# Turning the activated x tiles by DMA: 16-bit halves split on GpSimd, stored, and read back transposed

## The chip, the core and the metric

The kernel runs on one core of one Trainium2 chip. The metric is the device time in microseconds (us) of one execution. The kernel before takes 1605.04 us (median of 3 runs, 1604.93 to 1605.71).

## The reference, cut to what matters

The program is one layer: a layer norm, a state space mixer with a residual, a second layer norm, and a dense product with low-rank experts and a residual. Tokens: 2 batches of 512. The mixer has 128 heads of 64 features in 8 groups, and works in 4 chunks of 128 tokens.

```
proj = einsum('bsd,ed->bse', x, in_proj_w)          # gate | x, B, C | dt
hBC  = silu(causal depthwise conv with 4 taps(x, B, C))
xch  = hs * dt                                      # chunked, hs is the x part of hBC
Y_diag = einsum('bzlhn,bzshn,bhzls,bzshp->bzlhp', Cc, Bc, L, xch)
states = einsum('bzlhn,bhzl,bzlhp->bzhpn', Bc, decay_states, xch)
Y_off  = ...the states carried from chunk to chunk...
y = Y_diag + Y_off + hs * D ;  g = y * silu(gate) ; rms norm per group ; out projection
```

`proj` comes out with features on partitions and tokens along the row, since the convolution runs over tokens. `xch` is contracted over tokens, so `hs` has to be turned (tokens on partitions) before both `Y_diag` and `states`.

## The kernel before, in words

After a prologue of some 67 us the mixer runs 64 units, `k = 8 g + j`: group `g` of 8, unit `j` of 8, each unit 128 features (two heads) for both batches `b`. Every engine has its own instruction list, written out in order; semaphores join them. Each unit works one step ahead: while unit `k` is finished, the convolution of unit `k + 1` is made.

TensorE, in the order of its list for unit `k` (`body`, lines 878 to 955): the out products of banks 2 and 3 of unit `k - 1` (`later_outs`), the x projection of unit `k + 1` (`project` into `x_bank`), the chunk states of unit `k` (`states`, which wait for `xdecay`), the diagonal products (`diagonal`, which wait for `scores` and `xdt`), the gate projection of `k + 1`, the carried part (`carry`, which waits for `state`), the out products of banks 0 and 1 (which wait for `conv_ready` of unit `k + 1`), in units 4 and 5 of a group a projection of the next group's B or C, and then `turn_hs`: four 128 x 128 transposes for each batch, of `hs` of unit `k + 1`, into `head_bank`. The projections use products of a high and a low part, three for one.

VectorE, in the order of its list (`body`, lines 1357 to 1412): `to_heads` for both batches (line 1278: `xdt` is the turned `hs` times dt; it waits for `turned` and stands first in the unit), `add_outs` and the two `score` products, `y_low_part`, in units 1 to 3 `normed_out` (8 of them in a group), `tap(1)`, `carried_state` for both batches, `tap(2)` and `tap(3)` (which give `conv_ready` for unit `k + 1`), then `skip`, `carry_part`, `add_carry` (which give `y_sum`), and `add_outs`. In units 5 and 6 the taps of the next group's B and C (`bc_tap`) stand behind the first `add_outs`, and the scores of these units are made at the end of the unit before.

ScalarE: `tap0`, the high parts of the weights (`high_part`), the decays of the scores, `silu_hs` (line 1045: `hs_ready` for unit `k + 1`), the two gate activations, `finish`. In units 4 and 5 there is a third weight tile, whose high part stands behind the gate activations.

GpSimd: `decayed` for both batches (line 1469: `xdecay` from `xdt`), the low parts of the weights (line 1448), `add_squares`, the low part of the out weights, further low parts, and last `gated` for both batches, which waits for `y_sum`.

The SP queue issues every DMA, in the order of its list (`body`, lines 713 to 753): a weight tile, the out weights of unit `k + 1`, tables and columns in some units, weight tiles, `load_sums` for both batches, weight tiles, and `load_grown` (four DMAs, which wait for `y_sum` of unit `k`).

## Time and profile before

| what | value |
|---|---|
| median of the runs | 1605.04 us |
| span of the profiled execution | 1605.0 us |
| TensorE busy | 1583.5 us, 99% |
| VectorE busy | 1264.2 us, 79% |
| ScalarE busy | 1163.1 us, 72% |
| GpSimd busy | 700.7 us, 44% |
| DMA: mean busy share of 16 engines by the SP queue | 30.8% |

The profile is one execution. "Busy" is the time in which an engine has at least one instruction under way. The chain that ended last is followed back from the last instruction; its shares say which engine set the time. A timeline row gives the start in us from the span's start, the time from there to the end of the merged instructions, the engine, the line and operation, and in brackets how long the engine sat idle before it and who released it.

### The profile page before, as it was taken

The page shows a single profiled execution, that of the slowest core. Times are in us where ns is not written, and L with a number is a line of the kernel's source. Part 1 is how long each engine was busy: PE and PEld are TensorE (multiplying, and loading weights), DVE is VectorE, ACT ScalarE, POOL GpSimd, SP SyncE. Part 2 cuts the span into 40 slices and gives each one's busy share as a digit, 9 for nine tenths or more (in the row PEclk, how much of TensorE's full clock was granted, in tenths as well). Part 3 has the DMA queues.
Part 4 walks back from the last instruction along what each step waited for, and adds up shares of the span by engine and source line. Part 5 has one row for each costly group of instructions (what it writes and reads, how often), then busy time and mean ns, then how long its engine had stood idle before and what let it go on. Part 6 is the DMA issues. An engine that isn't in the chain of part 4 may idle for free.

```text
span 1605.0 us, 26714 instructions
## 1 busy us (share of the span) xinstructions
PE 1583.5 (99%) x9576; PEld 1346.1 (84%) x9576; DVE 1264.2 (79%) x1984; ACT 1163.1 (72%) x2027; POOL 700.7 (44%) x535
## 2 busy tenths in 40 slices
PE   7899999999999999999999999999999999999998
PEld 5688888888888888888888888888888888888887
DVE  6687777877778777887778877787877878788787
ACT  5887667776777677777687766777677767777753
POOL 2155444453444454354453544445344445435550
PEclk9999999999999999999999999999999999999999
DMA  4542322332323233332232232233232323223211
GB/s 151 192 145 86 122 89 83 112 112 73 112 97 114 73 109 95 98 106 92 99 108 97 86 122 89 83 112 112 73 112 99 113 73 109 99 92 112 93 44 53
DMA packets 86916, 162.37 MB, mean 101 GB/s; under 512 B 23040, under 2 KB 39424, under 8 KB 86528
## 3 DMA queue, kind: packets, MB, share of 16 engines
q1 hardware_dynamic: 86784, 160.66, 30.8%
q8 instruction: 77, 1.26, 0.3%
q14 instruction: 55, 0.45, 0.1%
HBM read 154.84 MB, written 5.77 MB: 100 GB/s over the span
## 4 chain that ended last, share of the span: by engine, by line
PE 97%; DVE 1%; ACT 1%; issue 0%; DMA 0%; SPq 0%; DVEq 0%; ACTq 0%
PE g_bank L778 10%; PE g_bank L780 9%; PE g_bank L779 9%; PE d_bank L797 7%; PE x_bank L778 7%; PE x_bank L780 7%; PE x_bank L779 7%; PE head_bank L786 5%; PE head_bank L804 5%; PE x_bank L836 4%; PE x_bank L837 4%; PE x_bank L835 4%; PE d_bank L837 4%; PE d_bank L835 4%; PE d_bank L836 4%; PE head_bank L812 3%
## 5 line engine op out<-in xcount | busy, mean ns | idle before, releaser
L1448 POOL TENSOR_TENSOR w_low<-raw,w_high 128x512 fp32r<-128x512 f32 x139 | 179.8, 1294 | 553.5 <-ACT w_high L1011 553.5
L1199 DVE SCALAR_TENSOR_TENSOR hs<-x_bank,cols,hs 128x1022 f32<-128x1022 f32 x189 | 241.6, 1278 | 129.7 <-ACT hs L1033 127.5
L1021 ACT ACTIVATE scores<-scores,tables 128x128 f32<-128x128 f32 x1024 | 312.4, 391 | 0.0
L1462 POOL TENSOR_TENSOR y<-y,gate 128x512 f32<-128x512 f32 x128 | 185.4, 1467 | 198.8 <-DVE y L1268 198.8
L1033 ACT ACTIVATE hs<-x_bank,cols 128x1024 f32<-128x1024 f32 x63 | 75.9, 1204 | 269.9 <-PE x_bank L780 269.9
L778 PE MATMUL g_bank<-x_high,w_high 128*128 128x512 f32 x624 | 250.8, 402 | 0.0
L779 PE MATMUL g_bank<-x_low,w_high 128*128 128x512 f32 x624 | 243.2, 390 | 0.0
L780 PE MATMUL g_bank<-x_high,w_low 128*128 128x512 f32 x624 | 243.1, 390 | 0.0
L778 PE MATMUL x_bank<-x_high,w_high 128*128 128x512 f32 x504 | 196.3, 390 | 0.1
L780 PE MATMUL x_bank<-x_high,w_low 128*128 128x512 f32 x504 | 196.1, 389 | 0.0
L779 PE MATMUL x_bank<-x_low,w_high 128*128 128x512 f32 x504 | 196.1, 389 | 0.0
L1231 DVE TENSOR_TENSOR scores<-scores,bc 128x1024 f32<-128x1024 f32 x128 | 169.0, 1327 | 4.3 <-ACT scores L1026 4.3
L778 PEld LDWEIGHTS g_bank<-x_high,w_high 128*128 128x128 f32 x624 | 117.0, 188 | 33.4 <-issue 11.0
L1469 POOL TENSOR_TENSOR xdecay<-xdt,tables 128x384 f32<-128x384 f32 x128 | 109.0, 873 | 78.4 <-DVE xdt L1278 78.4
L780 PEld LDWEIGHTS g_bank<-x_high,w_low 128*128 128x128 f32 x624 | 117.1, 188 | 25.3
L1026 ACT ACTIVATE scores<-scores 128x1024 f32<-128x1024 f32 x128 | 135.8, 1062 | 2.6
L779 PEld LDWEIGHTS g_bank<-x_low,w_high 128*128 128x128 f32 x624 | 117.2, 188 | 22.4 <-issue 0.2
L1456 POOL TENSOR_TENSOR square_sum<-square_sum,gate 128x1024 f32<-128x1024 f32 x55 | 133.0, 2419 | 3.3 <-DVE scores L1231 2.9
L1245 DVE SCALAR_TENSOR_TENSOR state<-state,chunk_tab,head_bank 128x64 f32<-128x64 f32 x512 | 121.0, 278 | 9.1
L797 PE MATMUL d_bank<-scores,xdt 128*64 128x128 f32 x2048 | 126.1, 276 | 0.0
L1256 DVE TENSOR_TENSOR grown_rows<-head_bank,grown_rows 128x384 f32<-128x384 f32 x128 | 71.4, 557 | 64.4 <-PE head_bank L804 57.3
L797 PEld LDWEIGHTS d_bank<-scores,xdt 128*64 128x64 f32 x2048 | 110.5, 137 | 7.9 <-issue 0.2
(211 smaller groups left out, 3433.3 us busy)
## 6 DMA issues: line engine op xcount, KB each, us to landing
scores<-sums_dram SPq DMA_DIRECT2D x128, 512.0 KB, 4.8
raw<-w_in SPq DMA_DIRECT2D x144, 256.0 KB, 2.9
grown_rows<-grown_dram SPq DMA_DIRECT2D x256, 96.0 KB, 2.8
out_raw<-w_out SPq DMA_DIRECT2D x64, 256.0 KB, 3.4
mixed<-x SPq DMA_DIRECT2D x8, 256.0 KB, 5.1
out<-mixed SPq DMA_DIRECT2D x8, 256.0 KB, 2.0
table_dram<-table SPq DMA_DIRECT2D x2, 768.0 KB, 5.3
tables<-table_dram SPq DMA_DIRECT2D x30, 48.0 KB, 2.7
```

What stands on the lines that cost most here:

```text
L778: pe.matmul(to, w_high[:, slot, k], x_high[:, b, k], start=(k == 0), stop=False)
L779: pe.matmul(to, w_high[:, slot, k], x_low[:, b, k], start=False, stop=False)
L780: mm = pe.matmul(to, w_low[:, slot, k], x_high[:, b, k], start=False, stop=(k == KT - 1))
L797: mm = pe.matmul(d_bank[r * HEAD_DIM:(r + 1) * HEAD_DIM, b, c * P:(c + 1) * P], xdt[:, b, c, r], scores[:, s, b, r, c], start=True, stop=True)
L835: pe.matmul(to, y_high[:, q, b, at], out_high[:, q], start=(i == 0), stop=False)
L1021: op = s.activation(at, at, ACT.Relu, bias=col[:, r, c:c + 1], scale=-1.0)
L1026: s.activation(scores[:, q % 2, b], scores[:, q % 2, b], ACT.Exp, scale=-1.0).then_inc(exp_ready, 1)
L1199: v.scalar_tensor_tensor(out=hs[:, q % 2, :, i:], in0=x_bank[:, :, 0:SEQ - i], scalar=cols[:, q, TAPS - 1 - i:TAPS - i], in1=hs[:, q % 2, ...
L1231: v.tensor_tensor(at, at, bc[:, b].rearrange("p c l -> p (c l)").unsqueeze(1) .to_broadcast([P, PAIR, SEQ]), ALU.mult).then_inc(scores_rea ...
L1448: pool.tensor_tensor(w_low[:, slot], raw[:, slot], w_high[:, slot].bitcast(F32), ALU.subtract)\
L1456: pool.tensor_tensor(square_sum[:], square_sum[:], gate[:, q % 2], ALU.add).then_inc(square_added, 1)
L1462: pool.tensor_tensor(y[:, b], y[:, b], gate[:, q % 2, b], ALU.mult).then_inc(y_ready, 1)
```

## The change

The eight TensorE transposes for each unit from unit 1 on are taken out; unit 0 keeps them (`turn_first`). In their place:

- GpSimd copies, behind the low parts of the weights and ahead of `gated`, for each batch the 512 fp32 words of `hs` of unit `k + 1` as two planes of 16-bit halves into `planes` (`planes_of`, 128 x 1024 16-bit elements each).
- SP stores each batch's planes to DRAM (`store_planes`, 256 KB), and after `load_grown` issues for each batch a transposing DMA (`turn_planes`, 256 rows of 512 16-bit elements in, 128 partitions of 4 x 256 out) that writes the turned fp32 words into `xdt`. It waits for the store, for `diag_done` and for `xdecay_ready` of unit `k`.
- VectorE's `to_heads` reads `xdt` and writes it in place; it waits for `xdt_in` and no longer for `turned`.
- `load_out` stands behind the stores and loads the tile for the unit after next.
- The wait for `carry_scaled` moves from `turn_hs` to `states`.
- `bias_high` and `bias_low` lie in space of `x_low` and `x_high` that is free by then; `bias_high` waits for the last projection.

```diff
+            def store_planes(k, b):
+                sp.wait_ge(planes_ready, BATCH * (k - 1) + b + 1)
+                reached(sp, xdt_in[b], 16 * (k - 1))
+                sp.dma_start(planes_dram[b], planes[:, b]).then_inc(planes_stored[b], 16)
+
+            def turn_planes(k, b):
+
+                sp.wait_ge(planes_stored[b], 16 * k)
+                sp.wait_ge(diag_done, BATCH * (k - 1) + b + 1)
+                sp.wait_ge(xdecay_ready, BATCH * (k - 1) + b + 1)
+                sp.dma_start_transpose(xdt[:, b].rearrange("p c r d -> p c (r d)").bitcast(U16),
+                                       planes_dram[b].rearrange("f h t -> (f h) t")).then_inc(xdt_in[b], 16)
...
-                    if ahead:
-                        load_out(ahead[2], (j + 1) % 2)
...
                     if ahead:
                         for b in range(BATCH):
+                            store_planes(ahead[2], b)
+                    if second:
+                        load_out(second[2], j % 2)
+                    if ahead:
+                        for b in range(BATCH):
                             load_grown(ahead[2], b)
+                        for b in range(BATCH):
+                            turn_planes(ahead[2], b)
...
             def states(k, b):
                 pe.wait_ge(xdecay_ready, BATCH * k + b + 1)
+                reached(pe, carry_scaled, BATCH * (k - 1) + b + 1)
...
-                    if ahead:
-                        for b in range(BATCH):
-                            turn_hs(k + 1, (j + 1) % 2, b)
...
             def to_heads(g, q, k, b):
                 if q % HALF == 0:
                     v.wait_ge(tables_in[b][q // HALF], 16 * (g + 1))
-                v.wait_ge(turned, BATCH * k + b + 1)
-                reached(v, diag_done, BATCH * (k - 1) + b + 1)
-                reached(v, xdecay_ready, BATCH * (k - 1) + b + 1)
+                if k == 0:
+                    v.wait_ge(turned, b + 1)
+                    hs_tok = head_bank[b].rearrange("p (c r d) -> p c r d", c=CHUNKS, r=PAIR)
+                else:
+                    v.wait_ge(xdt_in[b], 16 * k)
+                    hs_tok = xdt[:, b]
...
+            def planes_of(k, i, b):
+                pool.wait_ge(hs_ready, k + 1)
+                reached(pool, planes_stored[b], 16 * (k - 1))
+                pool.tensor_copy(planes[:, b], hs[:, i, b].bitcast(U16).rearrange("p (t h) -> p h t", h=HALVES))\
+                    .then_inc(planes_ready, 1)
...
                     for at in splits[1:]:
                         low_part(*at)
+                    if unit(g, last, j + 1):
+                        for b in range(BATCH):
+                            planes_of(k + 1, (j + 1) % 2, b)
                     for b in range(BATCH):
                         gated(j, k, b)
```

## Rows read from the trace of the kernel before

**Rows 1.** The page: busy times; granted TensorE clock, tenths, in 40 slices.
```profile
PE 1583.5 (99%) x9576; PEld 1346.1 (84%) x9576; DVE 1264.2 (79%) x1984; ACT 1163.1 (72%) x2027; POOL 700.7 (44%) x535
PEclk9999999999999999999999999999999999999999
```

**Rows 2.** The page: shares by engine of the chain that ended last.
```profile
PE 97%; DVE 1%; ACT 1%; issue 0%; DMA 0%; SPq 0%; DVEq 0%; ACTq 0%
```

**Rows 3.** Waits of TensorE, longest in total: us, times, longest.
```profile
PE x_bank L273 <- DVE xn L460: 8.6, 3, 5.7
```

**Rows 4.** Timeline of TensorE around the transposes of one unit.
```profile
670.85 1.03 PE L812 MATMUL head_bank<-ident,hs 128*128 128x128 f32 x8
671.64 0.48 PE L835 MATMUL d_bank<-out_high,y_high 128*128 128x512 f32 x1
```

**Rows 5.** Busy time of the engines in one group and in one unit.
```profile
670.85:861.40 190.55, 190.55 (x1168) 162.95 (x1167) 150.88 (x233) 139.99 (x244) 86.16 (x66) 1.00 0.30 99
671.64:693.68 22.04, 22.04 (x139) 18.82 (x138) 18.50 (x31) 16.91 (x31) 10.60 (x9) 1.00 0.30 102
```

**Rows 6.** Timeline of VectorE in that unit, from the end of its first step.
```profile
671.65 1.28 DVE L1278 TENSOR_TENSOR xdt<-head_bank,tables 128x512 f32<-128x512 f32 x2
673.31 0.69 DVE L1300 TENSOR_TENSOR acc<-d_bank,acc 128x512 f32<-128x512 f32 x1 [0.38 <-PE d_bank L837]
...
677.99 2.06 DVE L1304 SCALAR_TENSOR_TENSOR mixed<-acc,g_rstd,mixed 128x512 f32<-128x512 f32 x3
681.35 1.28 DVE L1199 SCALAR_TENSOR_TENSOR hs<-x_bank,cols,hs 128x1022 f32<-128x1022 f32 x1 [1.29 <-ACT hs L1033]
...
684.98 2.59 DVE L1199 SCALAR_TENSOR_TENSOR hs<-x_bank,cols,hs 128x1020 f32<-128x1020 f32 x2
```

**Rows 7.** Timelines of ScalarE and GpSimd in that unit.
```profile
681.22 1.14 ACT L1011 ACTIVATE w_high<-raw 128x512 fp32r<-128x512 f32 x2
...
687.60 1.06 ACT L1045 ACTIVATE hs<-hs 128x1024 f32<-128x1024 f32 x1 [0.52 <-DVE hs L1199]
688.57 1.10 ACT L1053 ACTIVATE gate<-g_bank 128x512 f32<-128x512 f32 x2
...
686.77 1.31 POOL L1448 TENSOR_TENSOR w_low<-raw,w_high 128x512 fp32r<-128x512 f32 x1
```

**Rows 8.** Timeline of the SP queue in that unit: DMA issues.
```profile
683.59 0.91 SPq L682 DMA_DIRECT2D scores<-sums_dram  x2
691.40 2.37 SPq L689 DMA_DIRECT2D grown_rows<-grown_dram  x4
...
694.45 0.43 SPq L678 DMA_DIRECT2D out_raw<-w_out  x1
```

**Rows 9.** DMA issues: count, KB each, median us from issue to landing.
```profile
out<-mixed SPq DMA_DIRECT2D x8, 256.0 KB, 2.0
...
tables<-table_dram SPq DMA_DIRECT2D x30, 48.0 KB, 2.7
```

**Rows 10.** DMA packets in the stretch 759.2 to 760.8 us, nearly all small.
```profile
DMA packets 374, 0.10 MB, mean 64 GB/s; under 512 B 361, under 2 KB 361, under 8 KB 374
...
q1 hardware_dynamic: 374, 0.10, 31.0%
```

**Rows 11.** The page: the SP queue's packets, MB, share of 16 engines.
```profile
q1 hardware_dynamic: 86784, 160.66, 30.8%
```

**Rows 12.** Groups of GpSimd instructions by line: busy us, mean ns.
```profile
L1456 POOL TENSOR_TENSOR square_sum<-square_sum,gate 128x1024 f32<-128x1024 f32 x55 | 133.0, 2419 | 3.3 <-DVE scores L1231 2.9 <-ACT gate L1074 0.4
...
L254 POOL TENSOR_SCALAR_AFFINE_SELECT ident<-ident 128x128 f32<-128x128 f32 x1 | 0.3, 292 | 0.1
...
L250 POOL MEMSET causal<- 128x128 f32 x1 | 0.2, 204 | 0.0
```

**Rows 13.** The engines around TensorE's idle time in the prologue; columns as in rows 5.
```profile
45.00:50.00 5.00, 1.11 (x8) 0.64 (x7) 4.89 (x5) 5.00 (x15) 0.00 (x0) 0.80 0.45 170
50.00:55.00 5.00, 4.81 (x12) 2.98 (x13) 0.52 (x1) 4.54 (x7) 0.00 (x0) 0.51 0.55 154
```

More of the change, by code:

```diff
@@ L9 @@
 F32R = mybir.dt.float32r
+U16 = mybir.dt.uint16
 ALU = mybir.AluOpType
@@ L21 @@
 PAIR = P // HEAD_DIM
+HALVES = 2
 GH = HEADS // GROUPS
@@ L97, in build @@
     dense_dram = scratch("dense_dram", [P, KT * HID])
+    planes_dram = nc.dram_tensor("planes_dram", [BATCH, P, HALVES, SEQ], U16, kind="Internal").ap()
     x_tokens = x.rearrange("b (c p) d -> p (b c) d", p=P)
@@ L134, in build @@
               conv_bc, unit_cols, w_out, bias, dense_dram, sums_dram, grown_dram, table_dram, chunk_dram,
-              out_tokens)
+              planes_dram, out_tokens)
 def prologue(nc, sem, banks, x_high, x_low, mixed, ident, causal, eps_col, buffers, loads, counts, x_tokens, w_dt,
@@ L619, in mixer @@
         chunk_tab = sb("chunk_tab", [P, BATCH, GH, CHUNKS])
+        planes = sb("planes", [P, BATCH, HALVES, SEQ], U16)
         ident_r = sb("ident_r", [P, P], F32R)
-        bias_high, bias_low = sb("bias_high", [P, HID], F32R), sb("bias_low", [P, HID], F32R)
+        bias_high, bias_low = x_low[:, 1, 0], x_high[:, 1, 0]
         g_std, g_rstd, squares = sb("g_std", [P, TB]), sb("g_rstd", [P, TB]), sb("squares", [P, TB])
@@ L626, in mixer @@
         out_raw_in = [sem(f"out_raw_in{i}") for i in range(2)]
+        planes_ready = sem("planes_ready")
+        planes_stored = [sem(f"planes_stored{b}") for b in range(BATCH)]
+        xdt_in = [sem(f"xdt_in{b}") for b in range(BATCH)]
         chunk_in = [[sem(f"chunk_in{b}_{h}") for h in range(2)] for b in range(BATCH)]
@@ L756, in _ @@
             load_out(0, 0)
+            load_out(1, 1)
             for b in range(BATCH):
@@ L806, in carry, with turn_first @@
                 mm.then_inc(carried, 1)
-            def turn_hs(k, s, b):
-                pe.wait_ge(hs_ready, k + 1)
-                reached(pe, carry_scaled, BATCH * (k - 1) + b + 1)
+            def turn_first(b):
+                pe.wait_ge(hs_ready, 1)
                 for c in range(CHUNKS):
-                    mm = pe.transpose(head_bank[b][:, c * P:(c + 1) * P], hs[:, s, b, c * P:(c + 1) * P], ident[:])
+                    mm = pe.transpose(head_bank[b][:, c * P:(c + 1) * P], hs[:, 0, b, c * P:(c + 1) * P], ident[:])
                 mm.then_inc(turned, 1)
@@ L859, in product_of @@
                     pe.wait_ge(bias_low_ready, 1)
-                pe.matmul(to, ident_r[:], bias_high[:], start=True, stop=False)
-                pe.matmul(to, ident_r[:], bias_low[:], start=False, stop=False)
+                pe.matmul(to, ident_r[:], bias_high, start=True, stop=False)
+                pe.matmul(to, ident_r[:], bias_low, start=False, stop=False)
                 pe.wait_ge(xt_ready, tb + 1)
@@ L895, in body @@
                                 pe.wait_ge(bc_ready, 1)
-                                turn_hs(0, 0, 0)
-                                turn_hs(0, 0, 1)
+                                turn_first(0)
+                                turn_first(1)
                     if j == 0:
@@ L1159, in body @@
                         s.wait_ge(bias_in, 16)
-                        s.activation(bias_high[:], bias_row, ACT.Copy).then_inc(bias_high_ready, 1)
+                        s.wait_ge(projected, BATCH * TILES)
+                        s.activation(bias_high, bias_row, ACT.Copy).then_inc(bias_high_ready, 1)
                         s.wait_ge(dense_in, 16)
@@ L1273, in to_heads @@
                     v.wait_ge(tables_in[b][q // HALF], 16 * (g + 1))
-                v.wait_ge(turned, BATCH * k + b + 1)
-                reached(v, diag_done, BATCH * (k - 1) + b + 1)
-                reached(v, xdecay_ready, BATCH * (k - 1) + b + 1)
+                if k == 0:
[4 more added lines that the diff above has]
+                    hs_tok = xdt[:, b]
                 col = table_of(DT, b, q).rearrange("p r c -> p c r")
-                v.tensor_tensor(xdt[:, b], head_bank[b].rearrange("p (c r d) -> p c r d", c=CHUNKS, r=PAIR),
+                v.tensor_tensor(xdt[:, b], hs_tok,
                                 col.unsqueeze(3).to_broadcast([P, CHUNKS, PAIR, HEAD_DIM]), ALU.mult)\
@@ L1498, in _ @@
             pool.wait_ge(bias_high_ready, 1)
-            pool.tensor_tensor(bias_low[:], bias_row, bias_high[:].bitcast(F32), ALU.subtract).then_inc(bias_low_ready, 1)
+            pool.tensor_tensor(bias_low, bias_row, bias_high.bitcast(F32), ALU.subtract).then_inc(bias_low_ready, 1)
             for k in range(KT):
```

2 lines of the change are left out of this document (1 added, 1 removed).

## The prediction, made before the changed kernel ran

> **What bounds the kernel now.** I read the page first, then the chain, then the timelines of one ordinary unit. TensorE is busy for 99% of the span at a granted clock of full speed in every slice [rows 1]; the chain that ended last lies on it for 97% [rows 2], and its longest wait in total, 8.6 us in three times, is for the prologue's norm [rows 3]. So in the 64 units each microsecond taken off TensorE counts, until something else is late. A group of 8 units takes 190.55 us, an ordinary unit 22.04 us, with TensorE busy in all of it and VectorE in 18.50 [rows 5]. The other engines wait for TensorE somewhere in each unit. What the reader should look for is how much room they have: the change sends the step from `hs` to `xdt` on a longer way, and this step closes a loop over GpSimd, SP, the DMA engines and VectorE.
>
> **What is removed.** The eight transposes of a unit start at 670.85 and the next product starts at 671.64 [rows 4]: 0.79 us of TensorE. They go from 63 units: 63 x 0.79 = 50 us. If nothing else were late, a unit would take 22.04 - 0.79 = 21.25 us, and the kernel 1605.0 - 50 = 1555. The profiled span and the median of the runs are the same to 0.1 us, so the sums below stand against both.
>
> **What is added, and where it lies.** In the kernel before, `hs` of unit k + 1 is ready at the end of line 1045 at 688.66 [rows 7], and TensorE turns it only at the end of the unit, some 4 us later; that wait costs nothing. After the change `xdt` of k + 1 is ready only after a chain of work, and `to_heads` stands first in VectorE's list: all that VectorE does for the unit (the scores, then `y_low`, the taps, the states) is queued behind it, GpSimd's `xdecay` waits for it, and TensorE's `states` and `diagonal` for both. The taps give `conv_ready`, without which there is no `hs` for the next unit. So there is a loop, from the end of one unit's `to_heads` to the end of the next one's, and its length is a floor under the unit. Its terms:
>
> (a) VectorE from the end of `to_heads` to the end of `tap(3)`, without its idle time: 673.31 to 677.99 is 4.68, and 681.35 to 687.57 is 6.22 [rows 6]: 10.9 us.
>
> (b) `silu_hs`, 1.06 [rows 7]; 1.1 with its start.
>
> (c) The copies on GpSimd, two, of 1024 elements each. No row has such a copy. From above: the sum of two operands of 1024 elements takes 2.42 us. From below: a memset of 128 elements takes 0.204 and the affine select, which reads one operand, 0.292 [rows 12]; eight times as many elements are at most 8 times that, and without the fixed part seen in the smallest instructions (about 0.1, an estimate) they give 0.95 and 1.65 for 1024. I take 1.4, between these two, since a copy reads one operand and does less than a select: 2.8 us for both. GpSimd is free then: its last low part ends at 688.08 [rows 7], so in an ordinary unit (c) starts at once. `gated`, queued behind it, waits for `y_sum` anyway.
>
> (d) SP's queue from the second store on: its issue 0.45 (half of two at 0.91), the out weights 0.43, then the four issues of `load_grown`, 2.37 [rows 8]: 3.25 us. These are ahead of the first transposing DMA. The second store needs 2.0 us to land (256 KB, `out`) [rows 9] and is hidden behind the 2.8 us that follow its issue. `y_sum`, for which `load_grown` waits, comes some 3.3 us after `tap(3)` by the same unit's order and is no later than the planes.
>
> (e) The two transposing DMAs. A small load (48 KB) lands 2.7 us after its issue [rows 9]. Their data: I assume packets of 256 bytes, a quarter of the 1024-byte rows that are read, since a transposing read has to be cut somewhere; then each DMA has 1024 packets, 64 to an engine. In a stretch with nearly only small packets, 374 took 31.0% of 16 engines in 1.6 us [rows 10]: 0.310 x 16 x 1.6 / 374 = 21 ns each, so 64 x 21 ns = 1.35 us. Over the whole span a packet took 0.308 x 16 x 1605 / 86784 = 91 ns, and a megabyte 49 us of one engine [rows 11]; by bytes 256 KB are 0.8 us, by packets at 91 ns 5.8 us. The two share the 16 engines, so the second lands at about 2.5 + 2 x 1.35 = 5.2 us after the first is issued. I take 1.35, since rows 10 is the nearest in packet size; 0.8 and 5.8 are the ends.
>
> The sum is 10.9 + 1.1 + 2.8 + 3.25 + 5.2 + 0.64 + 0.1 = 24.0 us. That is over 21.25 and over 22.04: TensorE is no longer the bound, and the 0.79 us taken off it are idle time.
>
> To a group this adds what VectorE or GpSimd puts into the loop in single units. `normed_out`: 8 x 0.69 = 5.5 [rows 6]. The reduction of the squares and the keeping of B times C: two operations of 1024 elements, 2.3 (by the 1.22 to 1.28 of VectorE's other operations of this size). In units 5 and 6 three taps of 1.25 come in and two scores of 1.15 go out of the loop: 2 x 1.4 = 2.8. In units 4 and 5 the third weight tile's low part is queued ahead of `planes_of` on GpSimd, and its high part on ScalarE behind the two gate activations: 1.1 + 0.6 + 1.3 = 3.0, and in unit 5 one activation of 1.0 more: 7.0 for both [rows 7]. A group is 8 x 24.0 + 5.5 + 2.3 + 2.8 + 7.0 = 209.6 us against 190.55: 19 more. Eight groups: 152. The first unit and the last have no such step, and the last group no B and C ahead, though its units before were the short ones too: about 5 less. 1605 + 152 - 5 = **1752 us**.
>
> **Edits at nothing.** `load_out` a unit earlier takes its load off nobody's path, since its issue stays in (d). The wait for `carry_scaled` at `states` is met: `carry_part` is over a whole projection earlier. The biases' new place costs at most the wait for the last projection, far ahead of the end product. The DMA engines: the stores by 33 MB and the reads by 33 MB on top of 160.66 [rows 11], 126 x 1.35 and 126 x 0.8 us, 17% of the span beside 30.8%; only collisions at the moment of (e) matter, and `load_grown` and the out weights are under way then, which can add some tenths.
>
> **Rivals.**
>
> 1. *TensorE stays the bound*: faster, 1555. The loop with 64 x 2.75 us less would fit 21.25. It needs both copies and both transposing DMAs in 2.8 + 2.7 - 2.75 = 2.75 us together, that is 0.7 us for a copy and 0.7 for a transposing DMA. The lower ends (0.95 and 0.8) give 3.5, and a group then gains 16 of the 19 us back: 1752 - 64 x 2.0 = 1624, still slower. For it: a copy of 16-bit elements may be quicker than rows of fp32 say; part of a batch's data may land beside the other's fixed time. Against it: every bound of (c) and (e) would have to be off at once. Chance 0.12.
>
> 2. *The transposing DMAs are far slower than plain ones of that packet size*: the upper end of (e), 5.8 us for each, adds 2 x 4.45 to each loop, 64 x 8.9 = 570: 2320 us. It decides from about 2.5 us a transposing DMA, where the total passes 1900. For it: the average packet of this trace costs 91 ns [rows 11], and the issue of such a DMA on SP may itself take longer than 0.45 us. Against it: most of these packets are 2 KB and more, and the small ones took 21 ns [rows 10]. Chance 0.17. The page on the three transpose paths is the one that speaks for it.
>
> 3. *TensorE's clock falls.* In the prologue TensorE was busy for 1.11 of 5 us, and the granted clock went to 0.80 and, in the next 5 us with work to do, to 0.51 [rows 13], about the level of 1.2 GHz. With a loop of 24.0 and 21.25 us of work, TensorE idles for some 3 us a unit, in one or two pieces at `states` and at the out products. If each brings 5 us at half the clock, 2.5 us of work are lost a unit, which the 2.75 us of idle time nearly cover; with the units' extras uncovered up to 64 x 2 = 130 us are added: 1880. Chance 0.07. The Trainium skill, page TensorE: Matmul & The Clock Gate, section Why this matters for your kernels, warns of idle gaps of this order between bursts; in rows 13 the trace agrees with it for a gap of nearly 4 us.
>
> 4. *The change does not do what it says*: the transposing DMA is written out as a copy of single elements, 131072 for a batch. At 21 ns over 16 engines that is 172 us a batch, and the kernel takes over 20 ms. Chance 0.01.
>
> **How the numbers follow.** The loop of 24 us has 0.61, rival 1 0.12, rival 2 0.17, rival 3 0.07, rival 4 0.01, and 0.02 is for a loop so near the old unit that nothing changes. The loop's own range is 1665 (copy 1.1, transposing DMA 1.0: 64 x 1.3 = 83 less) to 1865 (1.65 and 2.0: 64 x 1.8 = 115 more). The whole range reaches down past the lower ends of (c) and (e) to 1600 and up into rival 2 to 2050, to leave some 0.1 out on each side. Two executions of this kernel differ by 0.05%, and about 0.2% is what a measurement can tell from no change: faster 0.12, the same 0.02, slower 0.86.
>
> **What will show it.** In the profile after: TensorE's busy share near 90%, with waits at `states` for `xdecay` and at the out products for VectorE's taps; VectorE's largest wait at line 1278's successor, for the DMA into `xdt`, some 5 us a unit (24.0 less its 18.5 of work); `planes_of` at 1.4 us; the two transposing DMAs landing 3.9 and 4.8 us after their issues; units of 24.0 us, 209 to 210 for a group; `gated` not late. If TensorE is still busy all through with units near 21.25, rival 1 holds; if the landing of the transposing DMAs is over 7 us, rival 2; if the granted clock is below full in the units, rival 3. The prediction is wrong most easily in (c) and (e), which no row shows; each microsecond of either counts 128 times.

## The result and the profile after

The changed kernel takes 1923.82 us (median of 4 runs, 1921.85 to 1926.27) against 1605.16 for the kernel before: a ratio of 1.198, 95% interval [1.197, 1.200]. The prediction had 1752, with a range of 1600 to 2050. The sign was right and the time lies in the range, but the loss was forecast at 147 us and is 319: less than half of it was foreseen. That the time lies in the range is luck: the prediction's range for the loop itself ended at 1865, and the width up to 2050 was left for slow transposing DMAs, which did not come.

From the page of the changed kernel (columns as in rows 1, 2, 9 and 11; the group rows give busy us, mean ns, and the idle time before with what ended it):

```profile
span 1921.4 us, 26326 instructions
...
PE 1646.8 (86%) x9072; PEld 1344.4 (70%) x9072; DVE 1468.0 (76%) x1984; ACT 1155.3 (60%) x2027; POOL 991.9 (52%) x661
...
q1 hardware_dynamic: 237984, 226.74, 39.2%
...
DVE 25%; issue 22%; POOL 19%; SPq 13%; DMA 11%; PE 8%; ACT 2%; POOLq 0%; DVEq 0%; ACTq 0%
...
L1305 DVE TENSOR_TENSOR xdt<-xdt,tables 128x512 f32<-128x512 f32 x126 | 109.8, 871 | 368.1 <-DMA xdt<-planes_dram 368.1
...
L1494 POOL COPY planes<-hs 128x1024 uint16<-128x1024 uint16 x126 | 157.2, 1277 | 308.5 <-ACT hs L1068 308.5
...
L1239 DVE SCALAR_TENSOR_TENSOR y_low<-y,cols,y_high 128x1024 fp32r<-128x1024 f32 x63 | 172.7, 2741 | 0.0
...
xdt<-planes_dram SPq DMA_TRANSPOSE x126, 3.5
```

TensorE went from 99% busy [rows 1] to 86%, and its share of the last chain from 97% [rows 2] to 8%. The chain now runs over VectorE, GpSimd, SP and the DMAs: the loop of the prediction. VectorE waits for the transposing DMAs 368 us in all. So far this is what was forecast. The row that was not forecast is in the first line: VectorE has the same 1984 instructions as before and is busy for 1468 us instead of 1264 [rows 1]. `y_low` is one of them: 2741 ns on average, against 1.28 us in the median before.

One unit of the changed kernel, from the start of the second batch's `to_heads` to the same point a unit later (columns as in rows 5):

```profile
799.65:830.39 30.74, 24.35 (x125) 19.52 (x126) 24.52 (x30) 15.78 (x29) 16.32 (x11) 0.89 0.38 111
```

It takes 30.74 us against 22.04 before, and VectorE is busy in 24.52 of it against 18.50 [rows 5]. Its timeline in the next unit:

```profile
829.30 0.69 DVE L1305 TENSOR_TENSOR xdt<-xdt,tables 128x512 f32<-128x512 f32 x1 [5.32 <-DMA xdt<-planes_dram]
830.39 1.06 DVE L1305 TENSOR_TENSOR xdt<-xdt,tables 128x512 f32<-128x512 f32 x1 [0.41 <-DMA xdt<-planes_dram]
...
833.98 1.70 DVE L1255 TENSOR_TENSOR scores<-scores,bc 128x1024 f32<-128x1024 f32 x1
835.60 3.40 DVE L1239 SCALAR_TENSOR_TENSOR y_low<-y,cols,y_high 128x1024 fp32r<-128x1024 f32 x1
838.93 4.14 DVE L1331 SCALAR_TENSOR_TENSOR mixed<-acc,g_rstd,mixed 128x512 f32<-128x512 f32 x3
842.99 1.27 DVE L1223 SCALAR_TENSOR_TENSOR hs<-x_bank,cols,hs 128x1022 f32<-128x1022 f32 x1
```

and that of GpSimd in the same unit:

```profile
831.54 0.84 POOL L1502 TENSOR_TENSOR xdecay<-xdt,tables 128x384 f32<-128x384 f32 x1 [0.62 <-DVE xdt L1305]
833.30 1.29 POOL L1475 TENSOR_TENSOR w_low<-raw,w_high 128x512 fp32r<-128x512 f32 x1 [0.93 <-ACT w_high L1034]
834.54 3.38 POOL L1483 TENSOR_TENSOR square_sum<-square_sum,gate 128x1024 f32<-128x1024 f32 x1
837.87 2.29 POOL L1520 TENSOR_TENSOR out_low<-out_raw,out_high 128x512 fp32r<-128x512 f32 x1
840.11 1.75 POOL L1475 TENSOR_TENSOR w_low<-raw,w_high 128x512 fp32r<-128x512 f32 x1
```

Read the two side by side. The second `score` ends at 835.6, and only about 2.3 us later `square_sum` (2.41 us by itself [rows 12]) ends, at 837.9. About 1.1 us after that `y_low` ends. In this stretch the two engines finish their operations in turn, not together. `y_low` takes 3.40 us for 1.28, `mixed` 4.14 for 2.06 [rows 6], `out_low` 2.29 for about 1.3. The tap at 842.99, which reads one operand from a TensorE bank and one from SBUF, takes its 1.27 as before. In the kernel before, VectorE did its scores and `y_low` between 673.3 and 678.0 [rows 6], while GpSimd, from 674.06 on, sat idle for 7.85 us, waiting for ScalarE's high part of a weight tile:

```profile
681.91 1.28 POOL L1448 TENSOR_TENSOR w_low<-raw,w_high 128x512 fp32r<-128x512 f32 x1 [7.85 <-ACT w_high L1011]
```

Now both engines start when `xdt` has landed.

SP's queue between the copies and the transposing DMAs (columns as in rows 8):

```profile
820.67 1.65 SPq L690 DMA_DIRECT2D planes_dram<-planes  x2
822.37 0.42 SPq L685 DMA_DIRECT2D out_raw<-w_out  x1
822.85 2.38 SPq L709 DMA_DIRECT2D grown_rows<-grown_dram  x4
825.34 2.59 SPq L697 DMA_TRANSPOSE xdt<-planes_dram  x2
```

### The profile page after: what moved, and what is told of

Its sections match the earlier page's. It is cut to its first block, busy times and chain, and to the rows that moved or that the text cites. A ratio compares the mean times of both kernels' runs of the same rounds, so it can differ in the third digit from the quotient of the medians.

```text
span 1921.4 us, 26326 instructions
## 1 busy us (share of the span) xinstructions
PE 1646.8 (86%) x9072; PEld 1344.4 (70%) x9072; DVE 1468.0 (76%) x1984; ACT 1155.3 (60%) x2027; POOL 991.9 (52%) x661
## 3 DMA queue, kind: packets, MB, share of 16 engines
q1 hardware_dynamic: 237984, 226.74, 39.2%
## 4 chain that ended last, share of the span: by engine, by line
DVE 25%; issue 22%; POOL 19%; SPq 13%; DMA 11%; PE 8%; ACT 2%; POOLq 0%; DVEq 0%; ACTq 0%
DMA xdt<-planes_dram 10%; SPq L709 7%; DVE hs L1223 6%; POOL planes L1494 5%; DVE y_low L1239 4%; DVE scores L1255 4%; POOL w_low L1475 4%; POOL square_sum L1483 4%; SPq L697 4%; POOL out_low L1520 4%; DVE mixed L1331 3%; DVE state L1269 3%; DVE xdt L1305 2%; ACT gate L1076 2%; POOL xdecay L1502 1%
## 5 line engine op out<-in xcount | busy, mean ns | idle before, releaser
L1305 DVE TENSOR_TENSOR xdt<-xdt,tables 128x512 f32<-128x512 f32 x126 | 109.8, 871 | 368.1 <-DMA xdt<-planes_dram 368.1
L1068 ACT ACTIVATE hs<-hs 128x1024 f32<-128x1024 f32 x64 | 67.9, 1061 | 483.5 <-DVE hs L1223 482.1
L1494 POOL COPY planes<-hs 128x1024 uint16<-128x1024 uint16 x126 | 157.2, 1277 | 308.5 <-ACT hs L1068 308.5
L1475 POOL TENSOR_TENSOR w_low<-raw,w_high 128x512 fp32r<-128x512 f32 x139 | 222.0, 1597 | 175.3 <-ACT w_high L1034 175.3
L824 PE MATMUL d_bank<-scores,xdt 128*64 128x128 f32 x2048 | 148.7, 290 | 95.2 <-issue 65.9
L1255 DVE TENSOR_TENSOR scores<-scores,bc 128x1024 f32<-128x1024 f32 x128 | 209.2, 1636 | 26.5 <-ACT scores L1049 26.5
L1239 DVE SCALAR_TENSOR_TENSOR y_low<-y,cols,y_high 128x1024 fp32r<-128x1024 f32 x63 | 172.7, 2741 | 0.0
L1483 POOL TENSOR_TENSOR square_sum<-square_sum,gate 128x1024 f32<-128x1024 f32 x55 | 166.8, 3033 | 2.9 <-DVE scores L1255 2.9
L813 PE MATMUL head_bank<-xdecay,b_tok 128*128 128x128 f32 x768 | 113.8, 288 | 54.9 <-POOL xdecay L1502 49.3
L861 PE MATMUL x_bank<-out_high,y_high 128*128 128x512 f32 x256 | 113.4, 443 | 52.7 <-DVE hs L1223 52.7
```

The source lines that it names most:

```text
L824: mm = pe.matmul(d_bank[r * HEAD_DIM:(r + 1) * HEAD_DIM, b, c * P:(c + 1) * P], xdt[:, b, c, r], scores[:, s, b, r, c], start=True, stop=True)
L1239: v.scalar_tensor_tensor(out=y_low[:, q % RING], in0=y[:], scalar=norm_col[:, q:q + 1], in1=y_high[:, q % RING].bitcast(F32), op0=ALU.mult ...
L1255: v.tensor_tensor(at, at, bc[:, b].rearrange("p c l -> p (c l)").unsqueeze(1) .to_broadcast([P, PAIR, SEQ]), ALU.mult).then_inc(scores_rea ...
L1475: pool.tensor_tensor(w_low[:, slot], raw[:, slot], w_high[:, slot].bitcast(F32), ALU.subtract)\
L1483: pool.tensor_tensor(square_sum[:], square_sum[:], gate[:, q % 2], ALU.add).then_inc(square_added, 1)
L1494: pool.tensor_copy(planes[:, b], hs[:, i, b].bitcast(U16).rearrange("p (t h) -> p h t", h=HALVES))\
```

## The experiments

Theory A: the loop of the prediction sets the time, and its VectorE term is longer than forecast since VectorE's operations with two operands in SBUF and GpSimd's operations that read SBUF hold each other up, now that the late `xdt` starts both together. Theory B: the added DMA traffic slows VectorE and GpSimd. A third candidate was that the crossbar (what a transposing DMA has and a plain one has not) is itself the main cost. Ratios are against the kernel before, timed again beside each run (1605.6 to 1606.4 us), and have 95% intervals; the changed kernel's 1923.8 us, from which the differences below are taken, was timed once, for the result. The terms (a) to (f) are those of the prediction.

**e5_short_squares.**

```diff
-                pool.tensor_tensor(square_sum[:], square_sum[:], gate[:, q % 2], ALU.add).then_inc(square_added, 1)
+                pool.tensor_tensor(square_sum[:, :, 0:8], square_sum[:, :, 0:8], gate[:, q % 2, :, 0:8],
+                                   ALU.add).then_inc(square_added, 1)
```

> The changed kernel with add_squares on GpSimd cut to 8 of 512 columns (so the sums of squares are left out; every wait stays). Theory A (VectorE's operations with two operands in SBUF and GpSimd's reading operations hold each other up, now that both start after the late xdt): the 3.35 us of add_squares go out of GpSimd's row beside y_low in 55 units, y_low falls from 3.33 to 2.3 us or less, and the time by 1 to 3 us in each of these units: 1924 - 55 to 165, about 1810. Theory B (the added DMA traffic slows VectorE): y_low stays at 3.3 us; GpSimd idles 8.5 us later in each unit, so the time stays within 10 us of 1924.

Measured: 1860.9 us, ratio 1.158 [1.156, 1.160], 63 us under the changed kernel. Its groups by line:

```profile
L1239 DVE SCALAR_TENSOR_TENSOR y_low<-y,cols,y_high 128x1024 fp32r<-128x1024 f32 x63 | 105.0, 1667 | 0.0
...
L1483 POOL TENSOR_TENSOR square_sum<-square_sum,gate 128x16 f32<-128x16 f32 x55 | 50.3, 915 | 2.9 <-DVE scores L1255 2.9
```

`y_low` loses 68 us of busy time (172.7 to 105.0) when one GpSimd operation beside it is cut, and the kernel gets 63 us faster, although GpSimd has idle time later in each unit (in the changed kernel 8.49 us ahead of the copies at 819.61). That is at the low end of A's forecast and against B. (The cut operation leaves the sums of squares out.) The cut operation, 16 elements a partition, takes 915 ns on average and 212 at least: it now waits for `y_low`.

**e6_beside.** All the added work, with nobody waiting for its result; TensorE turns `hs` as before, and GpSimd's next copies wait for the transposing DMA, which now writes over `planes`.

```diff
-                sp.dma_start_transpose(xdt[:, b].rearrange("p c r d -> p c (r d)").bitcast(U16),
+                sp.dma_start_transpose(planes[:, b].rearrange("p h t -> p (h t)").rearrange("p (c n) -> p c n", c=CHUNKS),
...
+                    if ahead:
+                        for b in range(BATCH):
+                            turn_hs(k + 1, (j + 1) % 2, b)
...
-                if k == 0:
-                    v.wait_ge(turned, b + 1)
...
+                v.wait_ge(turned, BATCH * k + b + 1)
+                reached(v, diag_done, BATCH * (k - 1) + b + 1)
+                reached(v, xdecay_ready, BATCH * (k - 1) + b + 1)
```

> All the added work, but nobody waits for its result: the copies on GpSimd, the stores and the transposing DMAs stay at their places in the lists, the DMAs write over the planes tile instead of xdt, and TensorE transposes and VectorE reads its bank as in the kernel before. Theory A: VectorE and GpSimd keep their old rhythm, y_low stays at 1.28 and the scores at 1.22 us, and the time is 1605 to 1620. Theory B: y_low and the scores are stretched as in the changed kernel by the same DMA traffic, and the time is over 1650.

Measured: 1606.2 us, ratio 1.0002 [0.9993, 1.0011]. From its page and its rows by tile (a row gives ns minimum/median/maximum):

```profile
PE 1582.8 (99%) x9576; PEld 1345.5 (84%) x9576; DVE 1290.9 (81%) x1984; ACT 1162.8 (73%) x2027; POOL 843.2 (53%) x661
```

```profile
L1242 DVE SCALAR_TENSOR_TENSOR y_low<-y,cols,y_high x63: 1272/1277/2309, 87.2 to 1550.0; 128x1024 fp32r<-128x1024 f32 x63
```

The copies, the stores and the transposing DMAs cost no time where nobody waits, and `y_low` keeps its 1277 ns with all the added DMAs there (VectorE's busy time rises by 27 us, in the scores and in `add_carry`). What B needs is a `y_low` beside busy DMA engines. Here are one of e6_beside and the one of the changed kernel at 835.60 (columns as in rows 5; the last but one is the DMA engines' share):

```profile
697.34:698.61 1.27, 1.27 (x7) 1.07 (x6) 1.27 (x3) 0.00 (x0) 0.00 (x0) 1.00 0.93 253
```

```profile
835.60:839.00 3.40, 3.22 (x25) 2.68 (x26) 3.40 (x3) 2.82 (x4) 3.40 (x2) 1.00 0.97 334
```

The DMA engines are at 93% and 97%; GpSimd is idle in the first and busy all through the second. Only the second is stretched. Theory B falls. The run also shows that the whole loss lies in the waiting, with what the waiting does to the rhythm.

**e7_read_beside and e8_write_beside.** The kernel before with GpSimd operations added at one place.

```diff
+                    pool.wait_ge(scores_ready, BATCH * k + 2)
+                    for i in range(2):
+                        reached(pool, beside, 2 * k + i)
+                        pool.tensor_tensor(bias_low[:].rearrange("p (c l) -> p c l", c=CHUNKS),
+                                           causal[:].unsqueeze(1).to_broadcast([P, CHUNKS, P]),
+                                           causal[:].unsqueeze(1).to_broadcast([P, CHUNKS, P]), ALU.mult).then_inc(beside, 1)
```

> The kernel before, untouched but for two added GpSimd operations a unit, each of 512 columns with two operands read from SBUF (about 1.3 us, results unused), held until the unit's scores are done, so that they start beside VectorE's y_low, while no added DMA is there. Theory A: y_low goes from 1.28 to some 2.3 us in most units, and the added operations over 1.3 us; GpSimd and VectorE have room, so the time stays within 0.5% of 1605. Theory B (only DMA traffic stretches VectorE): y_low stays at 1.28.

```diff
+                    pool.wait_ge(scores_ready, BATCH * k + 2)
+                    for i in range(5):
+                        reached(pool, beside, 5 * k + i)
+                        pool.memset(bias_low[:].bitcast(F32), 0.0).then_inc(beside, 1)
```

> The same place in the kernel before, but five GpSimd memsets of 512 columns (about 0.5 us each), which write to SBUF and read nothing. Theory A (reading against reading): y_low stays at 1.28 us. If any GpSimd work beside it stretches VectorE, y_low grows as in e7_read_beside. The time stays within 0.5% of 1605 either way.

Measured: 1608.0 us, ratio 1.0014 [1.0004, 1.0023], and 1605.9, ratio 1.0003 [0.9993, 1.0012]. VectorE and GpSimd with the reading operations:

```profile
698.11 1.27 DVE L1216 SCALAR_TENSOR_TENSOR y_low<-y,cols,y_high 128x1024 fp32r<-128x1024 f32 x1
698.27 3.46 POOL L1484 TENSOR_TENSOR bias_low<-causal 128x512 fp32r<-128x512 f32 x2 [2.89 <-DVE scores L1232]
699.30 3.63 DVE L1305 SCALAR_TENSOR_TENSOR mixed<-acc,g_rstd,mixed 128x512 f32<-128x512 f32 x3
```

and with the memsets:

```profile
697.69 1.28 DVE L1216 SCALAR_TENSOR_TENSOR y_low<-y,cols,y_high 128x1024 fp32r<-128x1024 f32 x1
697.83 2.87 POOL L1484 MEMSET bias_low<- 128x512 f32 x5 [2.87 <-DVE scores L1232]
698.89 2.07 DVE L1305 SCALAR_TENSOR_TENSOR mixed<-acc,g_rstd,mixed 128x512 f32<-128x512 f32 x3
```

The expectation for `y_low` in e7 was wrong in one point: it starts 0.16 us ahead of the GpSimd operation and keeps its 1.27 us. It is the added pair that waits (3.46 us; one alone takes 1.05), and then `mixed`, which stands next: 3.63 us for 2.07. Beside memsets, which read nothing, nothing is stretched. So it is reading against reading, in these rows whoever starts first goes through, and no added DMA is needed for it. The Trainium skill, page SBUF — State Buffer, section Who interferes with whom, says the same: a VectorE instruction with two SBUF inputs shares a read port with GpSimd's reads, held for a whole instruction. The trace agrees, with 3.63 against 2.07 us.

**e4_plain_read.**

```diff
-                sp.dma_start(planes_dram[b], planes[:, b]).then_inc(planes_stored[b], 16)
+                sp.dma_start(planes_dram[b].rearrange("f h t -> f (h t)"),
+                             hs[:, k % 2, b].bitcast(U16)).then_inc(planes_stored[b], 16)
...
-                sp.dma_start_transpose(xdt[:, b].rearrange("p c r d -> p c (r d)").bitcast(U16),
-                                       planes_dram[b].rearrange("f h t -> (f h) t")).then_inc(xdt_in[b], 16)
+                sp.dma_start(xdt[:, b].rearrange("p c r d -> p (c r d)").bitcast(U16),
+                             planes_dram[b].rearrange("f h t -> f (h t)")).then_inc(xdt_in[b], 16)
```

> The changed kernel with a plain store of hs and a plain read of 256 KB into xdt in place of the transposing DMA (so the x tiles are not turned; the copies on GpSimd stay and all waits stay). It prices the crossbar. A plain 256 KB read lands 2.6 us after its issue, the second of a pair some 0.5 us later, against 3.5 and 5.1 for the pair now: the loop loses 1.5 to 2 us, 64 x 1.75 = 110: about 1815. If the crossbar is the main cost of the change, the time falls below 1720. If the crossbar costs nothing beyond a plain read, it stays within 30 us of 1924.

Measured: 1836.1 us, ratio 1.144 [1.142, 1.146], 88 us under the changed kernel. SP's issue and VectorE's next step:

```profile
816.47 0.99 SPq L698 DMA_DIRECT2D xdt<-planes_dram  x2
```

```profile
820.00 1.32 DVE L1306 TENSOR_TENSOR xdt<-xdt,tables 128x512 f32<-128x512 f32 x2 [5.04 <-DMA xdt<-planes_dram]
```

That is near the 1815 of the expectation. In this unit both batches are there 3.5 us after the first issue with a plain read, and 5.05 with the transposing pair (825.34 to 830.39). A single DMA lands 3.3 us after its issue in the median with the plain read and 3.5 with the transposing one, so most of the 1.5 us is SP's issue (2.59 for a pair against 0.99). Over all 63 units the stretch from the first issue to the end of `to_heads`, (e) and (f), is 68 us shorter, 1.1 a unit; the rest of the 88 us lies in VectorE's term (a), 901 us for 920, since the rhythm has moved too. With a plain read in this place 231 us of the loss remain: the crossbar is not the main cost.

**e1_turn_early.**

```diff
                         for b in range(BATCH):
                             store_planes(ahead[2], b)
+                        for b in range(BATCH):
+                            turn_planes(ahead[2], b)
                     if second:
                         load_out(second[2], j % 2)
                     if ahead:
                         for b in range(BATCH):
                             load_grown(ahead[2], b)
-                        for b in range(BATCH):
-                            turn_planes(ahead[2], b)
```

> The changed kernel with the two transposing DMAs issued ahead of the out weights and of the four DMAs of load_grown. The loop account (in both theories): between the end of the copies and the first transposing issue lie now 3.37 us of SP issues; after it the landing of the stores, 2.0 us for the second, and the first can go even sooner. 1.4 to 2.2 us less in each of 63 units: 1924 - 90 to 140, about 1810. If the loop does not run over SP, nothing changes.

Measured: 1718.9 us, ratio 1.070 [1.067, 1.072]: 205 us under the changed kernel, more than forecast.

```profile
701.49 1.65 SPq L690 DMA_DIRECT2D planes_dram<-planes  x2
703.49 2.59 SPq L697 DMA_TRANSPOSE xdt<-planes_dram  x2
```

The first transposing DMA goes 2.00 us after the first store, before the second has landed. In this unit it is 5.5 us from the end of the copies (702.78) to the second `to_heads` (708.31), against 8.4 in the changed kernel (821.97 to 830.39). Over all 63 units (d) and (e) together come to 381 us for 529: 148 us less, 2.35 a unit. I had counted from the second store alone. The rest, 52 us, is (a), 868 us for 920: the rhythms have moved again, and `y_low` has a median of 1.47 us (`mixed` is longer, 1.77 for 1.55).

**e2_heads_late and e3_both.** One new order of VectorE's list, with SP's as in the changed kernel (e2) and as in e1 (e3).

```diff
-                    for b in range(BATCH):
-                        to_heads(g, j, k, b)
                     if j == 1 and g > 0:
                         squares_of(g)
...
                     if scores_here:
                         score(g, j, k, 1)
+                    for b in range(BATCH):
+                        to_heads(g, j, k, b)
```

> The changed kernel with to_heads behind the two scores in VectorE's list; SP's list as in the changed kernel. The loop account: from the end of to_heads to the taps, the two add_outs and the two scores go out of the loop, 4.3 us of 30.7 by their own durations, and the scores no longer run beside xdecay: about 5 us less in 6 of 8 units, 3 less in the two with the scores elsewhere: 1924 - 63 x 4.5 = 1640. If the loop were not over VectorE's list but over GpSimd or DMA alone (a rival that the chain of the changed kernel, 19% GpSimd and 24% DMA and SP, would allow), the time stays above 1850.

> e1_turn_early (1719 us) and e2_heads_late together. The loop account: a further 4.5 us out of a loop of some 27.5 gives 23, and TensorE's 21.25 a unit is then near: 1560 to 1640, with TensorE busy over 96%. If y_low and normed_out, which still stand behind xdt beside GpSimd's readings, stay stretched to 3.3 and 2 us, the time is near the upper end.

Measured: e2 1684.7 us, ratio 1.049 [1.047, 1.051], 45 us above its forecast; e3 1594.6, ratio 0.993 [0.992, 0.995], inside its own. One move in VectorE's list gives 239 us of the 319 back, and with e1's the kernel is 0.7% faster than the kernel before. The scores do not need `xdt`; behind it they, with the two `add_outs`, had made the loop 4.3 us longer by their own durations and shared GpSimd's time. In e2 the term (a) falls by 324 us over the 63 units, but (e) grows by 60, since `to_heads` now stands behind the scores when the DMAs land, and (d) by 18: the expectation left that out.

**e9_third_later and e10_after_ylow.** The steps of e3_both's units, seen by the starts of `diagonal`: 21.3, 21.3, 21.3, 28.3, 28.3 us and so on; the ordinary ones are at TensorE's 21.25. Both runs start from e3_both. On SP e9 also puts the load of the third weight tile behind the transposing DMAs; the first cut is GpSimd's list.

```diff
-                    for at in splits[1:]:
+                    for at in splits[1:2]:
                         low_part(*at)
                     if unit(g, last, j + 1):
                         for b in range(BATCH):
                             planes_of(k + 1, (j + 1) % 2, b)
+                    for at in splits[2:]:
+                        low_part(*at)
```

> e3_both (1594.6 us), whose ordinary units take 21.3 us, as TensorE alone would, while units 4 and 5 of a group take 28.3 against 26.7 that TensorE needs (27.5 - 0.79). The account: in these two the third weight tile's low part stands ahead of the copies on GpSimd and its load ahead of the stores on SP, which costs 3 to 4 us of the loop. Here both stand behind. Expected: 28.3 falls to 26.7 to 27.2, 7 groups x 2 x 1.1 to 1.6 = 15 to 22 us less: 1573 to 1580. If these units are long for another reason (the taps of B and C on VectorE), nothing changes.

```diff
-                    for b in range(BATCH):
-                        to_heads(g, j, k, b)
                     if j == UNITS - 1 and not last:
                         keep_bc(g + 1, g_bank)
                     if prev and ahead:
                         y_low_part(prev[1], prev[2])
+                    for b in range(BATCH):
+                        to_heads(g, j, k, b)
```

> e9_third_later with to_heads also behind y_low_part. y_low then no longer runs beside xdecay, so both go back to their own durations (1.28 for 1.87, and 1.65 for the pair of xdecay in place of 3.0), and 1.3 us more go out of the loop; xdecay of the second batch is ready at about the same time after the scores. Expected 0 to 10 us below e9_third_later, from the units after the fourth; if xdecay comes later for TensorE's states, up to 10 us above.

Measured: 1594.7 us for e9 (ratio 0.993 [0.991, 0.994]), nothing gained; 1626.9 for e10 (1.013 [1.011, 1.015]), 32 us lost, three times what I allowed for. TensorE's `states` need `xdecay` early, and `y_low` ahead of it was too much: TensorE's wait for it rose from 26 to 46 us, and its busy time from 1545 to 1555. The trace of e9 shows what held the two long units:

```profile
580.29 0.69 DVE L1327 TENSOR_TENSOR acc<-d_bank,acc 128x512 f32<-128x512 f32 x1 [2.81 <-PE d_bank L863]
580.90 3.90 DVE L1232 SCALAR_TENSOR_TENSOR bc_conv<-g_bank,tap_bc,bc_conv 128x1022 f32<-128x1022 f32 x3
584.72 0.68 DVE L1327 TENSOR_TENSOR acc<-d_bank,acc 128x512 f32<-128x512 f32 x1
585.32 1.28 DVE L1305 TENSOR_TENSOR xdt<-xdt,tables 128x512 f32<-128x512 f32 x2
```

VectorE idles for 2.81 us, waiting for TensorE's `d_bank`. The two transposing DMAs are issued at 574.4 and 575.8 and land 3.4 and 3.8 us after their issues, by 579.6 at the latest. But the taps of B and C, 3.90 us, stand ahead of `to_heads`, which starts only at 585.32, 5.7 us after its data have landed.

**e12_heads_by_unit and e13_both_moves.**

```diff
                     if j in (5, 6) and not last:
+                        for b in range(BATCH):
+                            to_heads(g, j, k, b)
                         for i in range(1, TAPS):
                             bc_tap(i, 2 * (g + 1) + j - 5, j - 5)
...
-                    for b in range(BATCH):
-                        to_heads(g, j, k, b)
+                    if scores_here:
+                        for b in range(BATCH):
+                            to_heads(g, j, k, b)
```

> e3_both (1594.6 us), but in units 5 and 6 of a group, where the scores were made a unit earlier and the three taps of B and C (3.9 us) stand in their place, to_heads stands ahead of these taps: there the transposing DMAs land at about 0.8 us before VectorE's first add_outs, and TensorE waited for xdecay for 1.6 to 1.9 us a unit. Expected: 7 groups x 2 x 1.6 to 1.9 = 22 to 27 us less: 1568 to 1573, with TensorE's wait for xdecay (25 us) gone. If the units are then held by the copies behind the third weight tile, less than half of that.

> The same together with e9_third_later's two moves (which brought nothing alone: 1594.7). If the third weight tile is the next thing late in units 4 and 5, this one is up to 15 us faster than e12_heads_by_unit; if it has cover there, the two are the same within 3 us.

Measured: 1570.2 us, ratio 0.978 [0.977, 0.979], as forecast, and 1571.6, ratio 0.978 [0.977, 0.980]: the same, so that here the third weight tile has cover. From e12's page, and its wait of TensorE for `xdecay`:

```profile
PE 1536.1 (98%) x9072; PEld 1298.8 (83%) x9072; DVE 1328.2 (85%) x1984; ACT 1159.5 (74%) x2027; POOL 905.5 (58%) x661
```

```profile
PE head_bank L813 <- POOL xdecay L1505: 9.5, 5, 4.2
```

The long units are at 26.6 now (27.48 in the kernel before, less 0.79, is 26.7), the ordinary ones at 21.3. TensorE's busy time is 1583.5 - 1536.1 = 47 us under the kernel before, close to the 50 of the prediction, and 35 us of them arrive in the time of the kernel.

## Why the prediction was right in sign and wrong in size

**What is removed:** right. 50 us of TensorE, and e12_heads_by_unit, where TensorE is the bound again, shows 47.

**The loop:** right. It was named as the new bound, with its path over GpSimd, SP, the DMAs and VectorE, and moving its parts moved the time: e1_turn_early by 205 us, e2_heads_late by 239, e6_beside, in which it is open, by 318, that is by all of the loss.

**Its terms,** in the unit from 799.65 to 830.39 (one with `normed_out`, forecast 24.0 + 2.1 = 26.1 us, measured 30.7):

| term | forecast | measured | from |
|---|---|---|---|
| (a) VectorE, with `normed_out` | 10.9 + 2.1 | 17.8 | 800.65 to 818.46 |
| (b) `silu_hs` | 1.1 | 1.1 | 818.49 to 819.61 |
| (c) two copies | 2.8 | 2.4 | 819.61 to 821.97 |
| (d) SP | 3.25 | 3.4 | 821.97 to 825.34 |
| (e) transposing pair | 5.2 | 5.05 | 825.34 to 830.39 |
| (f) `to_heads` | 0.7 | 1.0 | 830.39 to 831.38 |

The two terms that no row showed, (c) and (e), on which the prediction put its doubt, came out within 0.5 us; the one that rested on rows failed.

The step that failed was: "VectorE from the end of `to_heads` to the end of `tap(3)`, without its idle time: ... 10.9 us". It took durations measured in one rhythm (VectorE's in [rows 6], with GpSimd idle for 7.85 us beside them) into another, in which GpSimd's `w_low`, `square_sum` and `out_low` run beside `score`, `y_low` and `mixed`. That is 4.8 us of this unit; in the next, whose rows stand above, (a) is the same 17.8 (831.38 to 849.19).

Over the kernel, VectorE's 1984 instructions are busy for 204 us more. By their own durations, which overlap a little, 90 of it lie in `y_low`, 40 in the scores and 37 in `mixed`, nearly all of these in (a), and 29 in `add_carry` and 24 in `to_heads`, which now reads both operands from SBUF. The forecast was 172 us short. Over the 63 units of the trace:

| term, 63 units | forecast | measured |
|---|---|---|
| (a), with the extras of the groups | 761 | 920 |
| (b) | 69 | 69 |
| (c), with the third weight tile | 225 | 208 |
| (d) | 205 | 221 |
| (e) | 328 | 308 |
| (f), with the hand-overs | 47 | 66 |

So (a) is 159 us over, and the others cancel. VectorE is idle for only 1.6 us in the 920, so the 159 are longer operations, not waits. The remaining 13 of the 172 are bookkeeping: by kinds of unit the forecast's own terms come to 1635 us for the 63 units, 160 over the 1475.5 that these took before, and not 147. That the engines hold each other up is shown by e5 (one GpSimd operation cut, 63 us), e6 (same DMAs, no stretch) and e7 against e8 (the kernel before).

**Within (e)** two misses nearly cancelled. I assumed 1024 packets of 21 ns for a transposing DMA; 1072 packets under 512 bytes came with each. The added packets are 151200 (237984 - 86784), 1200 for each store and read, and took 0.392 x 16 x 1921 - 0.308 x 16 x 1605 = 4140 us of engine time, 27 ns each. The issue of a transposing DMA takes 1.24 us on SP, not 0.45. But the second DMA landed sooner after its own issue: 3.7 us in this unit (3.5 is the median of all) instead of 4.8.
**Units 4 and 5:** the 7.0 us for the third weight tile were right in the changed kernel. In unit 28 (unit 4 of its group), where `silu_hs` ends at 876.89, the copies stand behind the tile's low part, and that behind ScalarE:

```profile
878.47 1.54 POOL L1475 TENSOR_TENSOR w_low<-raw,w_high 128x512 fp32r<-128x512 f32 x1 [6.38 <-ACT w_high L1034]
879.96 3.11 POOL L1494 COPY planes<-hs 128x1024 uint16<-128x1024 uint16 x2
```

The term (c) is 6.2 us in this unit and 6.8 in the next, 2.4 in an ordinary one: 8.1 more for both. In the order of e3_both the same tile has cover: moving it (e9_third_later, e13_both_moves) brought nothing, and the order of the taps and `to_heads` held these units.

**Rivals.** TensorE as the bound: not in this order, but e12 reaches it. Far slower transposing DMAs: no. The clock: it did fall, as rival 3 said. In the changed kernel, around TensorE's wait for `state` in one unit (columns as in rows 5):

```profile
842.60:845.53 2.93, 0.00 (x0) 0.00 (x0) 2.86 (x8) 0.00 (x0) 0.00 (x0) 1.00 0.32 89
845.53:848.40 2.87, 2.83 (x12) 2.24 (x12) 2.76 (x7) 0.00 (x0) 0.00 (x0) 0.60 0.00 0
```

After 2.9 us without work the granted clock averages 0.60 over the next stretch, so most of it ran at the lower level, 1.2 GHz, and `carry` takes 2.87 us there for 1.50 in the kernel before:

```profile
688.82 1.50 PE L804 MATMUL head_bank<-c_feat,state 128*128 128x128 f32 x12
```

TensorE's busy time is 113 us above 1583.5 - 50. But rival 3's sum does not hold: it charged this to the time, and the loop has room for it. The six terms of the table add up to all 1793 us of the 63 units, and none of them is work of TensorE. A late TensorE could show only as idle time of VectorE in (a), 1.6 us in all, or as a wait of SP in (d), which is 3.38 us in an ordinary unit and 221.4 - 63 x 3.38 = 8 us over that in all. So the clock has at most some 10 us of the 319. A granted clock below full, which the prediction named as the sign of rival 3, came here with the loop itself, which left TensorE idle; it did not tell the rival from the forecast.

**What the profile was to show:** units of 24 us and groups of 209 to 210 (24 to 31 and, behind the first group, 228 to 233 were seen), copies of 1.4 us (1.04 median, 1.28 mean), landing 3.9 and 4.8 us after the issues (3.9 and 3.7 in the unit above, 3.5 in the median of all), VectorE's wait of some 5 us a unit (5.7), TensorE near 90% (86), waiting for `xdecay` (49 us) and for the taps (53 us).

## What to carry to other kernels

A step with cover in the old schedule may stand first in an in-order list, and then its new latency is paid in full with all that is queued behind it: find the loop it closes, and before pricing the step look for work in that list that does not need it (here two moves in VectorE's list and one in SP's turned 1924 us into 1570, 2.2% under the kernel before). When a wait moves, durations move too: ask for each operation with two operands in SBUF on VectorE what GpSimd reads at that moment in the new order, not in the trace of the old. A transfer that nobody waits for can cost nothing even at 33 MB more each way (e6_beside): here the price of the change was its latency and what it did to the rhythm, not its bytes.

## What the runs showed of the hardware that was not expected

VectorE operations with two operands in SBUF and GpSimd operations that read SBUF go through one after the other wherever these traces show them side by side: `y_low` 1.28 to 3.33 us (median), `out_low` about 1.3 to 2.28, `mixed` 0.74 to 1.55. A GpSimd sum over 16 elements a partition took 1.20 us (median) behind `y_low`, and 0.21 alone. GpSimd's memsets stretched nothing. A copy of 1024 16-bit elements with a step of two takes GpSimd 1.04 us. A transposing DMA of 256 x 512 16-bit elements takes 1.24 us to issue and 3.5 to land, and with 126 of them beside plain DMAs on the same queue, and nobody waiting, the time stayed the same (e6_beside). The two engines' turns do not depend on the DMA engines: `y_low` took 1.27 us with these at 93% and GpSimd idle.
